# Loads of raw weight blocks and stores of their sums move from SyncE's queue to GpSimd's

## The reference, cut to what matters

```python
x = x + L0(...)            # Haar wavelet with a gate
x = x + L1(...)            # recurrence, h = tanh(x Wx + h Wh + b)
# L2, over 4096 tokens of 512 features:
for e in range(2):         # shared experts, inner width 1024 each
    h = silu(x_flat @ s_w1[e].T) * (x_flat @ s_w3[e].T)
    shared_out = shared_out + h @ s_w2[e].T
...                        # router, top 2 of 8, routed experts with gelu
x = x + (shared_out / 2 + routed_out) / 4
x = x + L3(...)            # gated leaky recurrence
```

## Time and profile before

| what | us |
|---|---|
| median of 3 runs | 1923.02 (1921.5 to 1924.93) |
| profiled execution, device time | 1924.83 |
| its span, first to last instruction | 1923.2 |
| TensorE busy | 1889.9 (98%) |
| VectorE busy | 1161.6 (60%) |
| ScalarE busy | 913.6 (48%) |
| GpSimd busy | 157.2 (8%) |
| part 0 of the shared experts | about 268 to 788 |

### The profile page before, as it was taken

The page is one execution under the profiler, slowest core; times in us unless marked ns, Lnnn a source line. Parts: engine busy times, 40 slices in busy tenths (PEclk is TensorE's granted clock), DMA queues, the critical chain, the costliest instruction groups (busy, mean ns, idle before and its releaser), DMA issues. The chain is left out here.

```text
span 1923.2 us, 46865 instructions
## 1 busy us (share of the span) xinstructions
PE 1889.9 (98%) x18676; PEld 1220.0 (63%) x18676; DVE 1161.6 (60%) x2541; ACT 913.6 (48%) x1939; POOL 157.2 (8%) x159
## 2 busy tenths in 40 slices
PE   8999989999999999999999999999999999999998
PEld 7999954444444434444444444457777777799997
DVE  6666646555688565412111115678877887688887
ACT  4444445424122344434333335534445554488886
POOL 0000000000000000122121102111111120000000
PEclk8999999999999999999999999999999999999999
DMA  7033337876453565799999967655554467233223
GB/s 309 14 131 131 132 139 190 228 210 196 144 176 121 197 201 182 166 258 204 225 217 198 208 142 240 188 165 167 147 169 138 138 163 245 75 112 90 47 47 58
DMA packets 307486, 312.94 MB, mean 163 GB/s; under 512 B 229416, under 2 KB 248494, under 8 KB 300399
## 3 DMA queue, kind: packets, MB, share of 16 engines
q1 hardware_dynamic: 294334, 267.01, 48.2%
q0 software_dynamic: 12960, 43.26, 9.6%
HBM read 190.93 MB, written 73.14 MB: 137 GB/s over the span
## 5 line engine op out<-in xcount | busy, mean ns | idle before, releaser
L1334 PE MATMUL sh_p<-xh,arena 128*128 128x512 f16 x1280 | 383.5, 381 | 7.4 <-ACT sh_gated L1610 4.8
L1405 PE MATMUL p<-sh_h_hi,arena 128*128 128x512 f16 x1024 | 304.6, 379 | 1.0 <-DVE sh_h_lo L1990 1.0
L1334 PE MATMUL sh_p<-xl,arena 128*128 128x512 f16 x640 | 244.1, 381 | 0.0
L2351 DVE SCALAR_TENSOR_TENSOR ro_hs<-ro_h,fac,ro_hs 128x512 f16<-128x512 f32 x71 | 53.4, 752 | 295.2 <-ACT ro_hs L2337 290.8
L1334 PEld LDWEIGHTS sh_p<-xh,arena 128*128 128x128 f16 x1280 | 125.7, 98 | 160.6 <-issue 5.9
L2294 PE MATMUL ro_py<-arena,ro_ht 128*128 x852 | 195.0, 379 | 0.0
L1405 PE MATMUL p<-sh_h_lo,arena 128*128 128x512 f16 x512 | 194.0, 379 | 0.0
L1581 ACT CAST sh_h_hi<-sh_gated 128x512 f16<-128x512 f32 x128 | 79.1, 618 | 234.4 <-DVE sh_gated L2083 207.7
L1405 PEld LDWEIGHTS p<-sh_h_hi,arena 128*128 128x128 f16 x1024 | 96.4, 98 | 106.7 <-DVE sh_h_lo L1990 1.7
L2294 PEld LDWEIGHTS ro_py<-arena,ro_ht 128*128 128x128 f16 x852 | 83.4, 98 | 100.5 <-issue 0.2
L2083 DVE SCALAR_TENSOR_TENSOR sh_gated<-sh_p,fac,sh_gated 128x512 f32<-128x512 f32 x80 | 59.9, 749 | 101.9 <-PE sh_p L1334 101.6
(11 more groups left out here) (335 smaller groups left out, 3960.5 us busy)
## 6 DMA issues: line engine op xcount, KB each, us to landing
stage<-in_shared_w SPq DMA_DIRECT2D x29, 768.0 KB, 5.3
routed_rows<-xres SPq DMA_DIRECT2D x71, 256.0 KB, 2.6
stage<-in_norms_r SPq DMA_DIRECT2D x16, 1024.0 KB, 4.9
stage<-in_routed_w SPq DMA_DIRECT2D x16, 1024.0 KB, 6.4
stage<-in_norms SPq DMA_DIRECT2D x14, 1024.0 KB, 5.0
arena<-x SPq DMA_DIRECT2D x12, 1024.0 KB, 5.7
x<-xres SPq DMA_DIRECT2D x16, 512.0 KB, 2.6
x_rows<-arena SPq DMA_DIRECT2D x8, 1024.0 KB, 9.0
```

The source lines that it names most:

```text
L1334: mm = nc.tensor.matmul(p1[u % P1][:], arena[:, w:w + P], x[slot(gl)][:, :, k, :], start=(j == 0), stop=(j == 3 * KD - 1))
L1405: mm = nc.tensor.matmul(p2[m][:], arena[:, w:w + P], h[n % 2][:], start=(i == 0 and j == 0), stop=(i == HID - 1 and j == 2))
L2351: nc.vector.scalar_tensor_tensor(hs[t % TURNS][:, D:2 * D], h[t % 2], fac[:, 3:4], hs[t % TURNS][:, 0:D], ALU.mult, ALU.subtract).then_inc ...
```

## The change

`load_mix` and `store_mix` go out of SyncE's list and into GpSimd's, unchanged in size and in what they wait for, but for one wait: a load now waits for `first(MIX_AT[t] - 1)` to be over (`p1_filled`). GpSimd issues load 0, store 0, load 1, store 1 and so on to store 8 (blocks with `MIX_AT` below 48), then its waits and four gathers as before, then load 9 to store 15. VectorE's and ScalarE's work on the blocks stays where it was.

```diff
@@ SyncE, shared_part, part 0
-                def load_mix(t):
-                    if t:
-                        sp.wait_ge(mix_lo, t)
-                    sp.dma_start(mix[:], src["shared_w"][t][:, 0:2 * PIECE]).then_inc(mix_in, 16)
-
-                def store_mix(t):
-                    sp.wait_ge(mix_lo, t + 1)
-                    sp.dma_start(dram["mixed"][t], mixed[:].rearrange("p s h n -> p (s h n)")).then_inc(mix_stored, 16)
...
-                    if first_part and n - 2 in MIX_AT:
-                        store_mix(MIX_AT.index(n - 2))
-                    if first_part and n in MIX_AT:
-                        load_mix(MIX_AT.index(n))
@@ GpSimd, shared_part, part 0
+                    def load_mix(t):
+                        pool.wait_ge(p1_filled, 2 * MIX_AT[t])
+                        pool.dma_start(mix[:], src["shared_w"][t][:, 0:2 * PIECE]).then_inc(mix_in, 16)
+
+                    def store_mix(t):
+                        pool.wait_ge(mix_lo, t + 1)
+                        pool.dma_start(dram["mixed"][t], mixed[:].rearrange("p s h n -> p (s h n)")).then_inc(mix_stored, 16)
+
+                    ahead = [t for t in range(HID) if MIX_AT[t] < (PART_GROUPS - 1) * HID]
+                    for t in ahead:
+                        load_mix(t)
+                        store_mix(t)
                     pool.wait_ge(listed, 1)
                     pool.wait_ge(xt_stored, 16 * LOOKS)
                     pool.wait_ge(p1_filled, 2 * (PART_GROUPS - 1) * HID)
                     for t in range(ROWS_RING):
                         nc.gpsimd.indirect_dma_start(row_ring(keep, t), None, dram["xt"], bass.IndirectOffsetOnAxis(ap=token_of[:, t:t + 1], axis=0)
                                                      ).then_inc(keep["rows_in"][t], 16)
+                    for t in range(len(ahead), HID):
+                        load_mix(t)
+                        store_mix(t)
```

## The result

| | before | changed |
|---|---|---|
| median of the runs | 1923.11 us (1921.5 to 1926.49, 20 runs) | 1925.85 us (1922.19 to 1929.53, 20 runs) |
| ratio, 95% interval | | 1.0013 [1.0007, 1.0019] |
| profiled execution (span) | 1924.83 (1923.2) | 1924.79 (1923.1) |

The changed kernel is slower by 0.13%, 2.7 us; the forecast was 1922.3, and the change moved the time to the other side. So the difference is looked for inside the stretch that the change touches, not in the spans.

The account below looks back on a forecast made before the run. TensorE, 98% busy, bounds the kernel; only its 7.02 us loss around block 10 could be won. Second layer of item 52 at 702.7 instead of 704.10 (-1.4), plus 0.7 for the clock: -0.7 us, 1922.3, range 1917.0 to 1927.5.

Parts of the forecast that it names:

- The first nine blocks at 0: Blocks 0 to 8, issued by GpSimd instead of SyncE: no cost or gain on TensorE, booked at 0.
- Load 9: On GpSimd behind store 8 and four gathers: starts at 666.9, lands after 6.4 us, VectorE waits 3.9.
- GpSimd's issue: Issuing on GpSimd: 0.85 us each plus 0.30 to the next, so a load starts 1.15 after the previous block's low half.
- e: Extra landing time of item 50's second-split 1 MB load beside store 9 and load 10: +1.2 us, bounds -1.8 and +3.0.
- Load 10: Block 10's load on GpSimd: starts at 682.05, wanted at 693.1, landing bounds 4.3 to 7.9 us, so cost 0.
- d: Delay of VectorE's block 9 sums waiting for their load, carried to the second split's load: 3.9 us, bounds 1.8 to 5.4.
- signs of being right: Block 9 waits 2 to 5 us, its load starts near 667, block 10's in time, TensorE gaps in pieces, blocks 0-8 untouched.
- Rival C: Full DMA engines: block 10's load takes 11.1 us wherever issued, hole and clock fall stay, about 1923.0; chance 0.15.
- A: Hole in items 50 to 53 closes, block 9's load landing near its lower bound: -5.4 us, 1917.6; chance 0.20.
- B: Block 9's load slowed further by GpSimd's queue and shared DMA engines, clock down behind it: +4.1 us, 1927.1; chance 0.15.
- The clock: TensorE's clock falling after its last wait in the hole: 0 to 2.6 us, taken as 0.7.
- Blocks 11 to 15 at 0: Later blocks' loads on GpSimd: 2.5 us of delay under 3.58 us of cover, so cost 0.

Follow-up runs that it names:

- best run: Changed kernel with load 9 issued ahead of the gathers, the third group's x store at item 50 and token-row transposes at item 59: 1916.89 us, ratio 0.9964.
- load 9 first: Changed kernel with GpSimd issuing load 9 ahead of the four gathers instead of behind them: 1920.85 us, ratio 0.9984 to the kernel before.
- both spacing edits: Kernel before, all blocks on SyncE, with the third group's x store at item 50 and token-row transposes at item 59: 1921.78 us, ratio 0.9985.
- x store at 55: Changed kernel with load 9 ahead of the gathers and the third group's x store at item 55 instead of 49: 1923.69 us, ratio 0.9999.
- x store at item 50: Changed kernel with load 9 ahead of the gathers and the third group's x store at item 50 instead of 49: 1918.07 us, ratio 0.9972.

## Why the prediction was wrong

*What bounds the kernel: held.* All that could be won was the 7.02 us of the hole. The best run agrees: it wins 7.0 (1923.86, the kernel before timed beside it, against 1916.89), and the spans less L1 and L2 show no other loss, to within 2.7 us. That the two figures meet so closely is luck, as the hole itself varies by more.

*The first nine blocks at 0: held*, by the run with only those blocks moved. VectorE's instructions took as long as before with GpSimd issuing beside them (0.42 and 1.28 us in the rows of both kernels).

*Load 9: held in every number.* It was to start at 666.9, land after 6.4 us and make VectorE wait 3.9; it started at 666.35 (667.07 on the time of the kernel before), landed after 6.5 and VectorE waited 4.10. On the Trainium skill's figure, "DMA: Bandwidth & Descriptors", section Specifications, the estimate had been 4.7 for a GpSimd load. The quickest of the 16 in the changed kernel took 4.5, 0.2 above SyncE's quickest where the page's two figures are 0.4 apart. So the trace does not contradict the page for an undisturbed load; this one was not undisturbed.

*GpSimd's issue: a little too dear.* Load 10 left 0.86 us after the low half of block 9 (680.47 to 681.33), not 1.15.

*The second split's matrix load: e was +1.2 and measured -0.2.* It landed in 6.2 us although store 9 and load 10 now ran beside it. It was issued 1.5 us ahead of them.

*Load 10: the step that failed.* The text said that its "bounds of 4.3 to 7.9 hold well within that, so it costs 0". The bounds were load 9's, carried over to a stretch with other traffic. It took 12.7 us and landed at 694.0; on the time of the kernel before that is 694.7, where the forecast had 690 at the latest. VectorE, which got there at 691.20, waited 2.85. From there the chain was right to the digit: 9.64 us from 694.05 to the end of the low half at 703.00 + 0.69 = 703.69, and the second layer at 703.75. Counted from the start of item 49, that layer came at 43.65 us; the forecast was 702.7 - 660.82 = 41.9, and before it was 43.28. So load 10 made the sum 1.8 us too low. The rows that warned of it were 11.1 us for this very load and a 1 MB load in 9.4 beside it; they were put down to the late issue and the dense traffic. They warned of the step, but not of its size: 682.05 + 11.1 = 693.15 would have met the 693.1 at which the load was wanted, and the sum would have stood. What the text left out is the 1 MB store of x. It stands right behind the second split's matrix load in SyncE's list, so it moved with d as that load did. Its rows in the kernel before, the issue and the landing:

```profile
676.21 0.43 SPq L1148 DMA_DIRECT2D x<-xres  x1
```

```profile
x<-xres SPq DMA_DIRECT2D x1, 1024.0 KB, 8.6
```

There it had landed at 684.8, so load 10, issued at 682.75, had it beside it for 2.1 us. In the changed kernel it left at 679.67 and landed at 689.7, and load 10 had it beside it for 8.3 us. Taking the store away gave back 1.7 us of landing in the first case (10.9 to 9.2, the kernel before) and 7.2 in the second (13.2 to 6.0, load 9 first, with 8.3 us side by side as well).

Most signs of being right had come: block 9's wait, the start of load 9, and gaps of TensorE in several pieces (the four shown add up to 6.2 us). Of these, only "load 10 in time" failed, and the largest gap, 3.00, is what it cost. So the right signs can come with the wrong time. Of the signs of being wrong, the waits at blocks 11, 14 and 15 came.

*Rival C was right in its mechanism and incomplete.* Load 10 was late wherever it was issued, 12.7 us after its issue where C had 11.1, because of what shared the DMA engines with it: without the store of x beside it, the same load took 6.0. The Trainium skill's rule, "DMA: Bandwidth & Descriptors", section "Issuing engines are not separate DMA queues", that DMAs of all issuers interleave on the same 16 engines, agrees with the 11.1 and 12.7 us from two issuers. My objection to C, that SyncE's list is long too, was also true: with both spacing edits, the issuer decides 4.5 to 4.9 us. The same page of the Trainium skill calls the time saved on the issuing side usually small; here GpSimd also spares the load its wait in SyncE's in-order list, and that is not small. Rivals A and B did not occur: d + e was 4.1 - 0.2 = 3.9, above A's 2.6 and below B's 6.5.

*The clock: 0.7 taken, 0 in the profiled execution*, some in the second profile (0.83 in 700 to 710). Two profiles of one kernel differ in it, so it was no term to take as certain.

*Blocks 11 to 15 at 0: failed, small.* The allowance was 2.5 us of delay under 3.58 of cover. VectorE waited 2.23 us for block 11 and 3.09 and 1.60 for blocks 14 and 15, where load 14 took 10.3 us beside the transposes. Cover used at one block is not there for the next. In the profiled execution L2 is 0.42; the run with later transposes takes 1.0 off the median.

*The balance.* The forecast was -0.7 us and the medians moved by +2.7. In the first profile load 10 is 1.8 of the difference and L2 0.4, while the clock's 0.7 did not come: together +0.8, which is L1 + L2 of the changed kernel (7.82) less that of before (7.02). Between the means of two profiles of each the change adds 1.2 us, while the medians lie 2.7 apart in the first timing and 1.5 in the second. The later transposes take 1.0 off the median, of which the profiled L2 is 0.3 to 0.4; so they may account for some 0.7 of the remainder. The profile with the x store at item 50 shows that a meeting of load 14 with them costs 3.6 us when it goes badly. That the changed kernel's higher runs, up to 1929.53, are such meetings is an inference: no profile of it caught a run above its median by more than 0.2 us. So it is shown why nothing was won; of the 1.5 to 2.7 us by which the changed kernel is slower, the profiles hold about half, and the rest stays open.

## What to carry to other kernels

Price a transfer that moves by what else is in flight at its new time, not by its size. The longest landing seen in that stretch is a place to start and not a bound, even where a late issue seems to explain it: 11.1 us had been seen, and 12.7 came. A delay also moves what stands behind it in the same list, here a 1 MB store onto the load. A second issuing engine helps when an in-order list holds the transfer back and no large transfer is in flight beside it at its new time; both have to be arranged, and here GpSimd with load 9 first gave 3.3 us against the kernel before, the spacing alone 2.5, and both 7.0. A large store that is not wanted soon belongs where nothing urgent is in flight, and whoever moves it has to see which transfer it meets next.

## What the runs showed of the hardware

- The size of a load says little, the 1 MB store beside it much: 13.2 us with it (load 9 first) and 6.0 without it (x store at 55), issued by GpSimd within 0.2 us of the same time. The landings of the changed kernel's 16 loads of 512 KB from GpSimd (the answer on their line, as in the earlier trace rows):

```profile
DMA to landing us min/median/max: 4.5/5.8/12.7
```

- Within GpSimd's queue the second of two 512 KB transfers landed some 5 us after the first beside a 1 MB store (685.2 and 690.3, load 9 first), and 1.2 us after it where that store was issued only at 680.96 (680.7 and 681.9, the best run). Turning the order round turned the landings round.
- GpSimd issued a plain store or load of these blocks in 0.53 to 0.70 us, not the 0.85 of its stores elsewhere, and load followed store after 0.57 without a pause; the fourth gather grew from 0.94 to 1.67 us when a plain load stood behind it and stayed at 0.95 when none did.
- Two token-row transposes took 13.4 us beside a matrix load, store 13 and load 14 (x store at 50), and 5.8 us one item later, beside matrix loads alone (the best run).
